# Layer norms of a one-core hybrid network: variance products in four column groups of the array, deviations by four chunks

## What is computed

```python
def _ln_t(v, eps=1e-5):
    m = jnp.mean(v, axis=-1, keepdims=True)
    s = jnp.var(v, axis=-1, keepdims=True)
    return (v - m) / jnp.sqrt(s + eps)
...
x = x + _L0_conv_ref(_gn(x), L0_conv_qkv_w, L0_conv_qkv_b, L0_conv_rpb, L0_conv_proj_w, L0_conv_proj_b, L0_conv_ln_g, L0_conv_ln_b)
x = x + _L1_conv_ref(_gn(x), L1_conv_w_qkv, L1_conv_w_kernel, L1_conv_b_kernel, L1_conv_w_proj, L1_conv_alpha, L1_conv_beta)
t = _to_tokens(x)
t = t + _L2_attn_ref(_ln_t(t), L2_attn_Wq, L2_attn_bq, L2_attn_Wk, L2_attn_bk, L2_attn_Wv, L2_attn_bv)
t = t + _L2_ffn_ref(_ln_t(t), L2_ffn_sigma, L2_ffn_phi, L2_ffn_M_u, L2_ffn_M_phi_plus, L2_ffn_M_phi_minus, L2_ffn_log_weights, L2_ffn_gumbel)
t = t + _L3_attn_ref(_ln_t(t), L3_attn_Wq, L3_attn_Wk, L3_attn_Wv)
t = t + _L3_ffn_ref(_ln_t(t), L3_ffn_router_w, L3_ffn_router_b, L3_ffn_expert_w, L3_ffn_expert_b)
```

## Time and profile before

| | us |
|---|---|
| median of 3 runs (lowest, highest) | 3212.29 (3210.49, 3217.34) |
| the profiled execution's own time | 3219.43 |
| its span in the trace | 3217.6 |
| busy: PE, DVE, ACT, POOL | 2938.9, 1928.4, 1414.4, 1066.1 |
| stage `l0`, first matmul to last scale | 536.6 to 588.4 |
| stage `la` | 907.9 to 949.1 |
| stage `sp`, first DMA to last instruction | 1012.1 to 1084.1 |
| stage `ca` | 2312.2 to 2354.8 |
| stage `ex` | 2970.1 to 3012.6 |

### The profile page before, as it was taken

How to read it: one execution, slowest core, us unless ns; L and a number is a source line. 1 busy time by engine, 2 the same in 40 slices (tenths; PEclk the granted TensorE clock), 3 DMA queues, 4 the chain that set the end, 5 groups by cost and what they waited for, 6 DMA issues and landing times. The chain is left out here.

```text
span 3217.6 us, 61524 instructions
## 1 busy us (share of the span) xinstructions
PE 2938.9 (91%) x23047; PEld 2310.9 (72%) x23047; DVE 1928.4 (60%) x3796; ACT 1414.4 (44%) x3058; POOL 1066.1 (33%) x1109
## 2 busy tenths in 40 slices
...
DMA packets 419407, 213.43 MB, mean 66 GB/s; under 512 B 326260, under 2 KB 398604, under 8 KB 417324
## 3 DMA queue, kind: packets, MB, share of 16 engines
...
...
## 5 line engine op out<-in xcount | busy, mean ns | idle before, releaser
L1748 DVE TENSOR_TENSOR sl_vl_slot<-sl_psV_slot,sl_vh_slot 128x512 fp32r<-128x512 f32 x1024 | 636.1, 684 | 380.9 <-ACT sl_vh_slot L1730 380.8
L1730 ACT ACTIVATE sl_vh_slot<-sl_psV_slot 128x512 fp32r<-128x512 f32 x1024 | 529.5, 605 | 512.2 <-PE sl_psV_slot L1685 510.7
L1703 PE MATMUL sl_psY_slot<-sl_vl_slot,sp_Mh_sp 64*128 64x512 f32 x2048 | 418.2, 389 | 0.8 <-DVE sl_vl_slot L1748 0.3
L1703 PE MATMUL sl_psY_slot<-sl_vh_slot,sp_Mh_sp 64*128 64x512 f32 x2048 | 415.5, 386 | 0.0
L1703 PE MATMUL sl_psY_slot<-sl_vh_slot,sp_Ml_sp 64*128 64x512 f32 x2048 | 415.5, 386 | 0.0
L1661 POOL TENSOR_TENSOR sl_fl_slot<-sl_f_slot,sl_fh_slot 128x512 fp32r<-128x512 f32 x256 | 336.7, 1315 | 20.4
L1659 POOL CAST sl_fh_slot<-sl_f_slot 128x512 fp32r<-128x512 f32 x256 | 166.4, 650 | 451.5 <-PE sl_psV_slot L1685 450.5
L2106 DVE TENSOR_TENSOR ca_ptl_ca<-ca_psT_ca,ca_pth_ca 128x512 fp32r<-128x512 f32 (+1 forms) x272 | 183.8, 676 | 167.2 <-ACT ca_pth_ca L2043 167.2
L2043 ACT ACTIVATE ca_pth_ca<-ca_psT_ca 128x512 fp32r<-128x512 f32 (+1 forms) x272 | 158.9, 584 | 182.4 <-PE ca_psO_ca L87 178.7
L1703 PEld LDWEIGHTS sl_psY_slot<-sl_vl_slot,sp_Mh_sp 64*128 64x128 f32 x2048 | 208.8, 184 | 37.3 <-issue 12.7
L1703 PEld LDWEIGHTS sl_psY_slot<-sl_vh_slot,sp_Mh_sp 64*128 64x128 f32 x2048 | 208.4, 184 | 24.5
...
## 6 DMA issues: line engine op xcount, KB each, us to landing
sl_f_slot<-filt_hat SPq DMA_DIRECT2D x1024, 64.0 KB, 2.2
na_v_na<-na_windows SPq DMA_DIRECT2D x128, 390.0 KB
...
sl_u_slot<-u_hat SPq DMA_DIRECT2D x128, 64.0 KB, 2.2
y_hat<-sl_y_slot SPq DMA_DIRECT2D x128, 64.0 KB, 1.8
...
```

The costliest lines, as they stand in the source:

```text
L1703: mm = e.matmul(psY[half][:, :], left[pl][rows, :], right[pr][rows], start=kc == 0 and k == 0 and x == 0 and z == 0, stop=kc == KC - 1 and ...
L1730: e.activation(v_out(0, n, q), bank(4 * n + q), ACT.Copy).then_inc(S["v_high"], 1)
L1748: e.tensor_tensor(v_out(1, n, q), bank(m), v_out(0, n, q), ALU.subtract).then_inc(S["v_split"], 1)
```

## The change

`variance` now uses 32 columns of the array for each of a chunk's four blocks: block j goes to the column group j, to the partitions 32j to 32j+31 of `psV`, and the window of `mean_row` (now 48 columns wide) places chunk c in row c, or 16 + c, where a second copy goes. So all 16 chunks of both batches have rows of their own, in 128 partitions, and the root, reciprocal and split work on 128 x 128 elements. The high part goes to `high` and the low or high part is chosen by partition with `second` (0 or -1). A deviation is taken for each group of GC chunks: 4 in the plain stages (four groups, q = 0 to 3, two PSUM tiles `psV`), all 16 at once in `sp`. `spread` runs LAG = 6 chunks behind `variance`, in `sp` after all of them. In `sp` DVE does `vector_mix` 3 before the norm, and POOL the first two `low` before it waits for it.

```diff
             def _(e):
                 if first:
                     e.wait_ge(S["const_loaded"], 48)
-                    rows = L // 128
-                    e.memset(T["mean_row"][:, 0:127], 0.0)
...
                 op.then_inc(S["pick_done"], 1)
-                rows = L // 128
-                e.memset(T["mean_row"][:, 0:127], 0.0)
-                e.memset(T["mean_row"][:, 128:255], 0.0)
-                e.memset(T["mean_row"][:, 127:128], 1.0 / C)
+                e.memset(T["mean_row"][:, :], 0.0).then_inc(S["mean_zero"], 1)
                 e.tensor_scalar(T["centre"][:, :], T["ident"][:, :], 1.0 / C, None, ALU.subtract)
-                e.tensor_tensor(T["pick_row"][:, :], T["ident"][:, 0:rows], T["ident"][:, rows:2 * rows], ALU.add)
+                e.wait_ge(S["mean_zero"], 1)
+                for at in (15, 31):
+                    e.memset(T["mean_row"][:, at:at + 1], 1.0 / C)
+                halves = T["ident"][:, :].rearrange("p (j z c) -> p z c j", j=TPC, z=2)
+                e.tensor_tensor(T["pick_row"][:, :].rearrange("p (c j) -> p c j", j=TPC), halves[:, 0, :, :], halves[:, 1, :, :], ALU.add)
+                e.tensor_reduce(T["second"][:, :], halves[:, 1, :, :], AX.XY, ALU.add).then_inc(S["mean_zero"], 1)
+                e.wait_ge(S["mean_zero"], 2)
+                e.tensor_scalar(T["second"][:, :], T["second"][:, :], -1.0, None, ALU.mult)
...
+    GC, LAG = (NC2, NC2) if beside else (4, 6)
+    NG = NC2 // GC
...
                 def variance(c):
-                    b, u = divmod(c, NCH)
+                    q, at = divmod(c, GC)
                     e.wait_ge(S["squared"], c + 1)
+                    if at == 0 and q >= 2:
+                        e.wait_ge(S["sd_done"], q - 1)
                     for j in range(TPC):
-                        t = u * TPC + j
-                        mm = e.matmul(psV[b][:, :], T["mean_row"][:, 127 - t:255 - t], sq[c % 3][:, j * 128:(j + 1) * 128],
-                                      start=(t == 0), stop=(t == NT - 1))
+                        mm = e.matmul(psV[q % 2][32 * j:32 * (j + 1), :], T["mean_row"][:, 15 - c:47 - c],
+                                      sq[c % 3][:, j * 128:(j + 1) * 128], start=(at == 0), stop=(at == GC - 1))
                     mm.then_inc(S["v_summed"], 1)
...
                     variance(c)
-                    if c >= NCH + 2:
-                        spread(c - NCH - 2)
-                for c in range(NCH - 2, NC2):
+                    if c >= LAG:
+                        spread(c - LAG)
+                for c in range(NC2 - LAG, NC2):
                     spread(c)
...
             @block.scalar
             def _(e):
+                def deviation(q):
+                    e.wait_ge(S["v_summed"], GC * (q + 1))
+                    e.activation(sd[q][:, :], psV[q % 2][:, :], ACT.Sqrt, bias=T["eps"][:, 0:1]).then_inc(S["sd_done"], 1)
+
...
-                    if c == NCH + 1 or c == NC2 - 1:
-                        b = c // NCH if c == NC2 - 1 else 0
-                        e.wait_ge(S["v_summed"], (b + 1) * NCH)
-                        e.activation(sd[b][:, :], psV[b][0:NT, :], ACT.Sqrt, bias=T["eps"][0:NT, 0:1]).then_inc(S["sd_done"], 1)
+                    if c >= GC and c % GC == 0:
+                        deviation(c // GC - 1)
+                deviation(NG - 1)
...
             @block.vector
             def _(e):
-                for b in range(B):
-                    e.memset(rows[b][64:128, :].bitcast(F32), 0.0)
+                def deviation_rows(q):
+                    e.wait_ge(S["sd_done"], q + 1)
+                    e.reciprocal(rstd[q][:, :], sd[q][:, :]).then_inc(S["rstd_done"], 1)
+                    e.wait_ge(S["rstd_done"], q + 1)
+                    e.tensor_copy(high[q][:, :], rstd[q][:, :]).then_inc(S["rows_high"], 1)
+                    e.wait_ge(S["rows_high"], q + 1)
+                    e.scalar_tensor_tensor(rows[q][:, :], high[q][:, :], T["second"][:, 0:1], rstd[q][:, :], ALU.mult, ALU.add)\
+                        .then_inc(S["rows_done"], 1)
...
                 if beside:
                     beside.vector_weights(e)
                     beside.vector_mix_direct(e)
-                    for i in range(3):
+                    for i in range(4):
                         beside.vector_mix(e, i)
...
+                for q in range(NG):
+                    deviation_rows(q)
+                    for c in range(q * GC, (q + 1) * GC):
+                        scale(c)
                 if beside:
                     beside.low(e, 1, 1)
...
         e.wait_ge(S["scaled_m"], 2)
         self.signs(e, 0)
+        self.low(e, 0, 0)
+        self.low(e, 0, 1)
         e.wait_ge(S["mix_done"], 5)
         self.signs(e, 1)
-        self.low(e, 0, 0)
-        self.low(e, 0, 1)
         self.low(e, 1, 0)
```

More of the change, by code:

```diff
@@ L708, in layer_norm_channels @@
 def layer_norm_channels(nc, T, src, dst, tag, affine=None, beside=None):
-    X, NT = T["X"], L // 128
+    X = T["X"]
     img = lambda c: src[:, c * CH:(c + 1) * CH]
@@ L763, in spread @@
                     for j in range(TPC):
-                        t = u * TPC + j
+                        t = c * TPC + j
                         mm = e.matmul(psR[c % 3][:, j * 128:(j + 1) * 128],
-                                      T["pick_row"][:, t:t + 1].to_broadcast([128, 128]), rows[b][:, :],
+                                      T["pick_row"][:, t:t + 1].to_broadcast([128, 128]), rows[c // GC][:, :],
                                       start=True, stop=True)
@@ L800, in _, with scale @@
             def _(e):
-                for b in range(B):
-                    e.memset(rows[b][64:128, :].bitcast(F32), 0.0)
+                def deviation_rows(q):
[6 more added lines that the diff above has]
+                        .then_inc(S["rows_done"], 1)
+                def scale(c):
+                    e.wait_ge(S["r_in_psum"], c + 1)
+                    e.wait_ge(S["centred"], c + 1)
+                    if affine:
+                        x = X[:, c * CH:(c + 1) * CH]
+                        e.scalar_tensor_tensor(zg[c % 2][:, :], centred(c), affine[0][:, 0:1], psR[c % 3][:, :],
+                                               ALU.mult, ALU.mult).then_inc(S["scaled"], 1)
+                        e.wait_ge(S["scaled"], c + 1)
+                        e.scalar_tensor_tensor(x, zg[c % 2][:, :], affine[1][:, 0:1], x, ALU.add, ALU.add)\
+                            .then_inc(S["z_done"], 1)
+                    else:
+                        e.tensor_tensor(dst(c), psR[c % 3][:, :], centred(c), ALU.mult).then_inc(S["scaled"], 1)
                 if beside:
```

49 lines of the change are left out of this document (10 added, 39 removed).

## The result

| | before | after |
|---|---|---|
| median (lowest to highest), 8 runs each | 3213.89 us (3210.49 to 3219.13) | 3200.39 us (3199.38 to 3208.07) |
| profiled execution's own time | 3219.43 us | 3199.38 us |

The change makes the kernel 13.5 us (0.38%) faster: ratio 0.9962, 95% interval 0.9951 to 0.9973. The forecast was 3186, 26.7 us less than before: the sign was right and the size was double. 3200 lies at the upper edge of the range.

The account below looks back on a forecast made before the run. PE was taken to bound the kernel (91% busy), with DVE's list setting `sp`. Gains of 13.2 (`la`, `ca`, `ex`), 5.8 (`l0`) and 7.7 (`sp`) sum to 26.7 us, so 3212.3 becomes 3186; range 3177 to 3201.

Parts of the forecast that it names:

- the 0.36 us of the block: In the loop: time from the first start of a chunk's `variance` to the next line, going back to wider tiles included.
- 0.10 for going in: In the loop: entering the narrow tiles costs 0.10 us, so 0.46 us a chunk replace 0.89.
- the first boundary: Plain stage: from `spread` 3 to `spread` 4 takes 2.9 us where 1.77 would do.
- the three gaps: Each plain stage: PE has three gaps, released by DVE's `rows`; a sign that the forecast is right.
- the removed half of `sp`'s norm: `sp`: eight scales between 1047.7 and 1064.2 and one deviation are gone or faster, the source of its 7.7 us gain.
- The rival of no concurrency: `variance`: column groups run one after the other, 0.63 us a chunk over forecast; total 3226 us, chance 0.04.
- the rival of a low clock inside the loop: Loop: PE granted 1.2 GHz, a chunk with `spread` 1.3 us or more above forecast; total 3228 us, chance 0.04.
- the full drain: Each tiling change waits for running work: 0.15 us more a chunk, boundaries 0.5 more; 3198 us, chance 0.15 (or dearer boundaries).
- the price of a chunk: Loop of the stages: a chunk takes 1.32 us without `spread` and 1.77 with it.
- the clock in the tails: `la`: end at 35.9 us, or some 37.5 with groups 2 and 3 at 1.2 GHz; gain taken near the middle, 4.4.
- POOL beside DVE: `sp`: POOL's two `low` slow DVE's sum 3 by 2.0 us, with bounds 0 and 4.
- the gain of `la`: Plain stage `la`: 4.4 us less, taken alike for `ca` and `ex`, 13.2 us in all.

Follow-up runs that it names:

- pairs_early: Changed kernel with each next group's deviation rows taken after the group's first scale, and two chunks' `variance` and `spread` done in pairs, with buffers reallocated; 3183.25 us, ratio 0.9897.
- wide_groups: Changed kernel with `variance` back to full-width products instead of column groups, keeping groups of four chunks and the new orders; 3213.39 us, ratio 0.9988 against the kernel before.
- pool_order_back: Changed kernel with POOL's order in `sp` as before: the first two `low` stand behind the second `signs` again; 3198.43 us, ratio 0.9943 against the kernel before.
- rows_early: Changed kernel with DVE computing the next group's deviation rows after a group's first scale, not its fourth; 3182.68 us, ratio 0.9895 against the kernel before.
- early_pool_back: Changed kernel with the next group's deviation rows after a group's first scale, and POOL's order in `sp` as before; 3175.84 us, ratio 0.9883 against the kernel before.
- groups_of_eight: Changed kernel with the column tiling kept but groups of eight chunks and `spread` ten behind in the four plain stages; 3195.37 us, ratio 0.9936 against the kernel before.

## Why the prediction missed by half

**What held.** The concurrency of the four column groups, the 0.36 us of the block, 0.10 for going in, the first boundary (2.9 against 2.95), the three gaps and what releases them, the removed half of `sp`'s norm, and the sign. The rival of no concurrency and the rival of a low clock inside the loop didn't come. The number lies where the full drain was put (3198), and inside the range, but by a sum of smaller things, so that is luck. What failed are three terms of the sum, each too small: the price of a chunk, the clock in the tails, and POOL beside DVE.

**The step of the loop, 1.32 and 1.77 against 1.41 and 1.86.** The step of the prediction was that the 0.36 us of `fold_heads` "includes going back to wider tiles". It includes a part. I read the distance from one row's start to the next and not what the next row then did; and the next row there is a product of 64 columns, not one of the full width. A way in and out costs 0.33 us (`pairs_early`), and 0.10 of it lies inside the first wide product behind, where no distance between starts of rows shows it. 0.09 us a chunk makes `spread` 8 start at 28.6 instead of 27.4 in `la`: 1.2 us in `la`, `ca` and `ex`, and 0.5 in `l0`, where DVE sets the pace from the first `spread` on. That is some 4 us. The Trainium skill (TensorEngine Tiling (Array Packing), Key Properties) says that a change of the mode drains TensorE. The trace agrees that there is a price, and it is less than the drain to the recorded ends that I had as a rival, 0.15 more a chunk.

**The clock, taken at the middle where it was at its end.** I had 35.9 us for `la` at 2.4 GHz and 37.5 with two groups at 1.2 GHz, and took about the middle, though the change itself puts three gaps into PE's list. The 37.5 is also too low by my own prices: two ways to DVE at 1.15 for 0.70 and seven scales at 0.85 for 0.63 add 2.4, which makes 38.3. The clock did fall, just behind the second gap. With the gaps filled `la` takes 37.1, without 39.3; the former is the forecast for the high clock plus the 1.2 of the loop, and the latter is 38.3 plus the 1.2, less 0.45 for the first scale of the third group, which still came at the high price, plus 0.2 for a `variance` at the low one. So `la`'s shortfall of 2.5 is 1.2 of loop and 1.3 of clock. The four plain stages are 8.1 us shorter from the first `variance` on with the gaps filled, of which my middle had allowed some 0.9 a stage in three of them and 0.5 in `l0`: 4.9 us were missing.

**The beginnings.** I gave `ca` and `ex` the gain of `la`, though `la` alone begins at the high clock. That cost nothing in `ca` (4.2 us before and after), and in `ex` it hid 1.6 us of the miss by luck. In `l0` the beginning took 0.8 more than I had.

**POOL beside DVE in `sp`.** The term of 2.0 us was half of what it had to be. I put it on sum 3 and it fell on sum 2, which makes no difference: in `wide_groups` the two `low` did run beside sum 3, and sum 3 took 9.9 us there where I had 5.9 for it alone. The price of the two `low` beside a sum is 4.0 to 4.1 (`pool_order_back` against the change, `rows_early` against `early_pool_back`), which was my upper bound. Of the 2.2 that `sp` lacks, 2.0 are this and 0.2 the later landing of the matrix, whose cause is open. The three steps alone (9.81 for 7.84) would make it 2.0 and look like my term; the rest stands in the instruction ahead of them (2.56) or, in `rows_early`, behind them (3.25). The Trainium skill (SBUF — State Buffer, Who interferes with whom) says that an instruction of VectorE with two SBUF inputs contends with one of GpSimd that reads SBUF, and that the contention is an exclusive lock. The trace agrees: beside POOL's subtractions of 3.3 us a step of 1.28 us starts every 3.28, while the scales, which read PSUM and one SBUF operand, stay at 0.69 beside POOL. So two steps beside the two `low` cost 2 x (3.3 - 1.3) = 4.0, and I had the rows for it.

**The sum of the miss.** Of the 12.0 us between forecast and measured stages, the loop is 4, the clock 4.9 and `sp` 2.2, less 0.8 for the beginnings of `l0` and `ex` together. Some 1.6 us are left that no run assigns.

**What the sum hid.** Each boundary was costed rightly at 2.9 against 1.77, and I summed its price as part of the change. That it was a cost of DVE's order and not of groups of four (`groups_of_eight` wins 9.9 us, `rows_early` 24.7 in the five stages) was not seen as a question at all.
